# Loads of block boundaries in smaller pieces, ring places as remainders, and two waits removed in a graph network kernel

## The reference, cut to what matters

```python
for _ in range(3):
    msgs = relu(h[src] @ W_edge + b_edge)
    agg = segment_sum(msgs, dst, num_segments=50000)
    h = relu(concatenate([agg, h], axis=-1) @ W_agg + b_agg)
x = layernorm(x + h)
x = layernorm(x + attention_block(x, edge_index, edge_attr))
```

## Time and profile before

| | |
|---|---|
| runs, median | 4235.06 us (3 runs, 4228.87 to 4235.15) |
| the profiled execution, its own time | 4238.96 us |
| its span | 4236.9 us |
| mean granted clock of PE | 0.965 |
| PE busy (share of the span) | 3680.3 us (87%) |
| DVE busy | 3217.1 us (76%) |
| POOL busy | 2887.9 us (68%) |
| ACT busy | 2265.9 us (53%) |

### The profile page before, as it was taken

How to read it: one execution, slowest core, us unless ns; L and a number is a source line. 1 busy time by engine, 2 the same in 40 slices (tenths; PEclk the granted TensorE clock), 3 DMA queues, 4 the chain that set the end, 5 groups by cost and what they waited for, 6 DMA issues and landing times. The chain is left out here.

```text
span 4236.9 us, 101656 instructions
## 1 busy us (share of the span) xinstructions
PE 3680.3 (87%) x19764; PEld 2414.0 (57%) x19765; DVE 3217.1 (76%) x11124; ACT 2265.9 (53%) x4904; POOL 2887.9 (68%) x2867
## 2 busy tenths in 40 slices
PE   5777769999989999799998588888888779999998
PEld 3555548888778877677777244444444334444443
DVE  6888856667656766577777488888888659999998
ACT  1333325555545555455565344545454358777776
POOL 3777757777377766477662677777777377777775
PEclk8999979999999999999999899999999889999999
DMA  2555547888678877588776455555555334444443
GB/s 83 181 174 172 174 141 239 243 238 241 195 214 241 245 227 227 176 254 260 248 252 195 137 157 158 154 160 153 160 153 160 92 103 128 129 129 129 129 130 94
DMA packets 583567, 749.60 MB, mean 177 GB/s; under 512 B 146958, under 2 KB 407786, under 8 KB 583398
## 3 DMA queue, kind: packets, MB, share of 16 engines
q1 hardware_dynamic: 476774, 554.65, 40.2%
q0 software_dynamic: 106624, 193.25, 18.5%
HBM read 426.01 MB, written 321.54 MB: 176 GB/s over the span
## 5 line engine op out<-in xcount | busy, mean ns | idle before, releaser
L797 POOL DMA_INDIRECT mp_gathered<-msg_rows,other_idx x784 | 755.1, 963 | 354.8 <-issue 196.4
L1091 POOL DMA_INDIRECT ll_gathered<-msg_rows,other_idx x392 | 373.4, 953 | 216.3 <-issue 108.0
L815 PE MATMUL bank<-mp_edge_hot,mp_gathered 128*128 128x256 bf16 x3528 | 477.2, 276 | 36.7 <-POOLq L785 19.0
L559 POOL DMA_INDIRECT by_window<-so_pay,so_pos_i x392 | 387.5, 989 | 166.6 <-issue 112.8
L1679 POOL DMA_INDIRECT ff_agg<-at_rows,last_idx x392 | 382.9, 977 | 115.8 <-issue 106.9
L1383 POOL DMA_INDIRECT at_of_dst<-x_rows,node_idx x392 | 375.6, 958 | 119.5 <-issue 119.2
L1379 POOL DMA_INDIRECT at_of_src<-x_rows,kv_idx x392 | 370.9, 946 | 119.3 <-issue 111.7
L871 ACT ACTIVATE mp_h_out<-bank,mp_b_agg 128x256 f32<-128x256 f32 x392 | 185.9, 474 | 482.3 <-PE bank L833 472.9
L815 PEld LDWEIGHTS bank<-mp_edge_hot,mp_gathered 128*128 x3528 | 347.0, 98 | 107.5 <-issue 64.1
L904 DVE TENSOR_SCALAR mp_edge_hot<-digits,mp_first_col,column 128x256 bf16<-128x256 bf16 x1176 | 340.7, 355 | 67.0 <-issue 54.7
L1791 PE MATMUL bank<-ff_h_cols,ff_w 128*128 128x512 f32 x784 | 371.1, 596 | 0.9 <-ACT ff_h_cols L1824 0.9
(11 more groups left out here) (252 smaller groups left out, 8886.1 us busy)
## 6 DMA issues: line engine op xcount, KB each, us to landing
msg_rows<-mp_msg_out SPq DMA_DIRECT2D x392, 192.0 KB
mp_h_in<-h_cols SPq DMA_DIRECT2D x392, 128.0 KB
h_cols<-mp_h_out SPq DMA_DIRECT2D x392, 128.0 KB
msg_rows<-so_msg_out SPq DMA_DIRECT2D x98, 384.0 KB
h_cols<-so_h_out SPq DMA_DIRECT2D x98, 256.0 KB
ll_h_in<-h_cols SPq DMA_DIRECT2D x196, 128.0 KB
x_rows<-ll_x SPq DMA_DIRECT2D x98, 256.0 KB
skip_rows<-ll_skip SPq DMA_DIRECT2D x98, 256.0 KB
```

Source lines behind the costliest of these rows:

```text
L559: pool.indirect_dma_start(core.by_window, bass.IndirectOffsetOnAxis(ap=pos_i[k][:, t:t + 1], axis=0), pay[k][:, t, :], None, bounds_check= ...
L797: pool.indirect_dma_start(gathered[:, r * PARTS * D:(r + 1) * PARTS * D], None, core.msg_rows[layer % 2], bass.IndirectOffsetOnAxis(ap=cor ...
L815: product = nc.tensor.matmul(agg_bank[k], gathered[:, bass.ds(at + d * D, D)], hot, start=(first and d == 0), stop=True, skip_group_check= ...
L1091: pool.indirect_dma_start(gathered[:, r * PARTS * D:(r + 1) * PARTS * D], None, core.msg_rows[(LAYERS - 1) % 2], bass.IndirectOffsetOnAxis ...
```

## The change

In edge_tiles of both stages the load takes two words instead of eight, and is made at every second block instead of at every eighth. In add_tile of both the place in the ring is written as a remainder, i % 32, instead of i & 31. The wait of PE at L825 and the one at L1119 and L1120 are taken out. edge_tiles is called by PE's sum_edges and DVE's hots, so the loads change on both engines; add_tile is PE's alone.

```diff
--- before.py
+++ after.py
@@ -714,11 +714,11 @@
 
         def edge_tiles(eng, n, r):
 
-            if r == 0:
+            if r % 2 == 0:
                 words[eng.engine] = nc.values_load_multi_w_load_instructions(
-                    core.spans[0:1, bass.ds(n, MSGS)], engines=[eng.engine], min_val=0, max_val=512 * NT - 1,
+                    core.spans[0:1, bass.ds(n, 2)], engines=[eng.engine], min_val=0, max_val=512 * NT - 1,
                     skip_runtime_bounds_check_because="both halves are masked and only address tables of their size")[1]
-            word = words[eng.engine][r]
+            word = words[eng.engine][r % 2]
             return word & 511, word >> 9
 
         def further(eng, n, first, last, more):
@@ -810,7 +810,7 @@
                     wins, turns_done = layer * NW, layer * (NW // RING)
 
                     def add_tile(k, i, hot, first=False):
-                        at = (i & (TILES - 1)) * (PARTS * D)
+                        at = (i % TILES) * (PARTS * D)
                         for d in range(PARTS):
                             product = nc.tensor.matmul(agg_bank[k], gathered[:, bass.ds(at + d * D, D)], hot, start=(first and d == 0),
                                                        stop=True, skip_group_check=True)
@@ -822,7 +822,6 @@
                             pe.wait_ge(more_hot_ok[layer], at + 1)
                             add_tile(r % 2, i + 1, more_hot[:, bass.ds((at & 1) * W, W)]).then_inc(tile_mm[layer], 1)
                         first, final = edge_tiles(pe, n, r)
-                        reached(pe, h_ok, wins + n - 1)
                         pe.wait_ge(edge_hot_ok, wins + n + 1)
                         pe.wait_ge(tile_in, layer * NT + first + ALWAYS)
                         for c in range(ALWAYS):
@@ -1017,11 +1016,11 @@
 
         def edge_tiles(eng, n, r):
 
-            if r == 0:
+            if r % 2 == 0:
                 words[eng.engine] = nc.values_load_multi_w_load_instructions(
-                    core.spans[0:1, bass.ds(n, TURN)], engines=[eng.engine], min_val=0, max_val=512 * NT - 1,
+                    core.spans[0:1, bass.ds(n, 2)], engines=[eng.engine], min_val=0, max_val=512 * NT - 1,
                     skip_runtime_bounds_check_because="both halves are masked and only address tables of their size")[1]
-            word = words[eng.engine][r]
+            word = words[eng.engine][r % 2]
             return word & 511, word >> 9
 
         def further(eng, n, first, last, more):
@@ -1116,8 +1115,6 @@
                     pe.wait_ge(more_hot_ok, at + 1)
                     add_tile(r, i + 1, more_hot[:, bass.ds((at & 1) * W, W)]).then_inc(tile_mm, 1)
                 first, final = edge_tiles(pe, n, r)
-                if r % 2 == 0:
-                    reached(pe, sums_ok, Q * j + r // 2 - 1)
                 pe.wait_ge(edge_hot_ok, n + 1)
                 pe.wait_ge(tile_in, first + ALWAYS)
                 for c in range(ALWAYS):
```

## The result

| | median us | runs | against before, 95% interval |
|---|---|---|---|
| before | 4231.97 | 4224.97 to 4235.15 (4) | |
| after | 4257.14 | 4253.00 to 4259.77 (4) | 1.0061 [1.0043, 1.0078] |

A forecast was written before the change was run, and what follows sets the result against it. PE was taken as the bound in message passing, stopped at heads by its sequencer, which was late throughout the last layer. Gains of 65 us in message passing and 11 in the last layer gave 4159 us, range 4118 to 4212.

The forecast's parts named there:

- the load: PE and DVE: a two-word load at every second block takes 0.32 us, set between one and four words.
- The ends, 0.30 and 0.85: Lower and upper bound, in us, that the prediction gave its 0.32 for a two-word load.
- The thin cover: Rival: loads of 0.5 to 0.6, dearer remainder or gathers; half the heads' loss stays, last layer gains nothing; 4200; chance 0.12.
- loads above 0.5: Sign that the forecast is wrong: register loads taking more than 0.5 us, where some 0.32 was expected.
- The remainder: Ring place on PE: joins sum and products, five ALU_OPs fewer, 0.04 per longer FUSED_REGOPS; net 0.345 us a block off the sequencer.
- DVE takes over in the last layer: Last layer: DVE's turn becomes 22.2 us, later than PE's 20.9; the turn falls only 0.45 from 22.65, gaining 11 us.
- PE's turn there, put at 20.9: Last layer, four pairs of blocks: 22.65 - 8 x 0.345 - 0.9 + 4 x 0.48 = 20.9 us.
- The waits: The two removed PE waits are implied by earlier ones: 0, between 0 and 0.1 us a block of sequencer time.
- No change, since a load costs 0.6 whatever its words: Rival: DVE's last-layer turn 23.4, 18 us slower there, message passing some 20 faster; chance 0.05.
- The lead: Message passing: PE's sequencer runs 1.1 us ahead of the matmuls; no more was counted on. Rival that it grows: chance 0.05.
- The estimate of above 4 us from the 64 entries: PE's queue of 64 entries would allow a sequencer lead of 1.7 blocks, above 4 us; no row showed it.
- The heads: Message passing, every eighth block: PE's loss falls from 1.46 to 0.1 us at 24 heads, 33 us a layer.

## Why the prediction was wrong

- **The failed term is the load: 0.32 us forecast, 0.82 measured on PE in message passing, 0.53 on DVE in the last layer.** I set two words between one word and four, as if the price rose with the number. The four words lay on a whole piece, the two never do. The ends, 0.30 and 0.85, held the value; I took the wrong neighbour, and the range of the sum didn't carry the upper end through. The thin cover (chance 0.12) came nearest in mechanism, with loads of 0.5 to 0.6 and no gain in the last layer, and "loads above 0.5" was named as a sign of being wrong; but that rival kept half of message passing's gain.
- With 0.82 the prediction's own working gives the result. Message passing: 2 x 2.16 + 0.82 + 0.16 = 5.30 a pair, with a fourth of the branch 5.4, against PE's 5.02: 1.5 us a turn, as much as the one stop of 1.46 before. The last layer: 21.25 - 0.70 + 4 x (0.53 + 0.10) = 23.07; measured 23.16. Of the 0.50 that was missed on PE, 0.21 leads up to 0.53, about the least that two words take, and 0.29 is what they took beyond it, from a cause that stays open (last section). With 0.53 the same working gives an estimate of 5.11 a pair, a stop of 0.36 a turn: message passing would still have gained.
- **The remainder** was right: a FUSED_REGOPS grows by some 0.055 us (0.04 forecast), and alone it is worth 86 us.
- **DVE takes over in the last layer**: right. With PE's loads as before and DVE's changed that layer takes 570.7; with four words on PE and eight on DVE 531.6. But PE's loads alone hold it at 559.1, so PE's turn there, put at 20.9, was too short by the same term.
- **The waits**: taken as nothing, 5 us in fact.
- **No change, since a load costs 0.6 whatever its words** (chance 0.05) came nearest in time. But its mechanism is wrong too: eight words cost 0.61 or 3.2 by where they start.
- **The lead**: I counted on 1.1 us. With eight words at the head and remainders PE's sequencer gets further ahead. One block of that kernel, its FUSED_REGOPS and then its matmuls:

```profile
L815 PEldq FUSED_REGOPS  x9: 46/46/106, 1024.8 to 1025.9; - x9
...
L815 PE MATMUL bank<-mp_edge_hot,mp_gathered x9: 272/272/273, 1026.7 to 1027.6; 128*128 128x256 bf16 x9
```

1.9 us, and the three blocks before it have the same: further it doesn't get. By the rows, what stops it here is a wait of the kernel. In messages PE waits for ACT's relu of the edge products (L874), and the sequencer goes on to the next block 0.06 us after that relu has ended, at 212 of the 392 blocks of message passing. Before the block above, the relu ends at 1024.40, and the sequencer's first row of that block (L825) starts at 1024.5:

```profile
1023.93 0.47 ACT L874 ACTIVATE mp_msg_cols<-bank,mp_b_edge 128x256 f32<-128x256 f32 x1 [0.18 <-PE bank L837]
...
L825 PEldq ALU_OP  x1: 36/36/36, 1024.5 to 1024.5; - x1
```

The estimate of above 4 us from the 64 entries that the Trainium skill gives (Advanced Engine Details and Errata, Engine Queue Depths) is not put to the test by this, since the wait comes first. The heads still cost 0.56 us (3.07 in the median instead of 2.51) with eight words, where 0.1 was forecast, and 0.09 (2.60) with four.

## What to carry to other kernels

Count the instructions that a sequencer must get through per block as one counts an engine's work: PE, 95% busy, was still held by its own, and some 0.35 us a block off it was worth 2%. Load table words into registers in groups that start on 16 bytes and hold four words or a multiple, as far as these runs go (one to eight words); a load split to spread its cost may cost more in sum. When a price is read off a neighbouring row, ask in what else than size the two differ.

## What the runs showed of the hardware

The shortest load of words into registers in any of the runs (ns, PE and DVE) by words and start:

| words | starts on 16 bytes: PE, DVE | 8 bytes beside: PE, DVE |
|---|---|---|
| 1 (any place) | 296, 297 | |
| 2 | 532, 524 | 530, 519 |
| 4 | 328, 338 | 997, 960 |
| 8 | 587, 594 | 1930, 1841 |

On DVE 0.30 + 0.22 for each further word gives 0.52, 0.96 and 1.84 (PE's further word is 0.23); whole pieces cost 0.33, and 0.26 for a second. For loads of registers from HBM the Trainium skill (Runtime: NRT & Kernel Launch, Instruction fetch mechanics) gives some 200 ns a register, in bulk too. The 0.22 of these loads from SBUF is near that; the whole pieces, 0.26 for four registers, aren't.

Above these floors the spread is wide. PE's two-word loads in the last layer of the changed kernel take 538 in the median at its start (the first eight, to 1786.5 us) and 875 after it; DVE's stay at 521 to 558. That a busy engine delays its own sequencer's loads would fit this. It doesn't fit the kernel before with only the loads changed: there PE is at work beside 97 of the 98 loads of the last layer, and yet they stay near the floor in the median:

```profile
L1021 PEldq TENSOR_LOAD <-spans x98: 530/546/1651, 1856.4 to 2476.2; - x98
```

No run took the cause by itself, and it stays open.
